# A decoder layer and a gated cross attention on one core: the row sums' spread in one transfer, one step that opens with the values, one copy a quarter earlier

## The reference

```python
# layer 0, hidden x, encoder ctx
q, k, v = split(layernorm(x, ln1) @ w_qkv + b_qkv)          # phase A, 16 heads of 32
x = x + merge(softmax(q k^T / sqrt(32) * mask - 10000 (1 - mask)) v) @ w_ao + b_ao
q = layernorm(x, ln2) @ w_q + b_q;  k, v = split(ctx @ w_kv + b_kv)     # phase B
x = x + merge(softmax(...) v) @ w_co + b_co
x = x + gelu(layernorm(x, ln3) @ w1 + b1) @ w2 + b2         # MLP
# layer 1
a = layernorm(ctx, ln_gamma, ln_beta)
Q, K, V = x @ Wq.T, a @ Wk.T, a @ Wv.T                      # phase D
x = x + tanh(gate) * (merge(softmax(where(mask, Q K^T / sqrt(32), -inf)) V) @ Wo.T)
```

## Time and profile before

| | us |
|---|---|
| median of 3 runs | 1096.38 (1095.52 to 1099.59) |
| profiled execution | 1098.87 |
| its span, first to last instruction | 1097.2 |
| TensorE busy | 1068.6 (97%) |
| VectorE busy | 818.4 (75%) |
| ScalarE busy | 705.3 (64%) |
| GpSimd busy | 481.8 (44%) |

### The profile page before, as it was taken

The page is one execution under the profiler, slowest core; times in us unless marked ns, Lnnn a source line. Parts: engine busy times, 40 slices in busy tenths (PEclk is TensorE's granted clock), DMA queues, the critical chain, the costliest instruction groups (busy, mean ns, idle before and its releaser), DMA issues.

```text
span 1097.2 us, 24221 instructions
## 1 busy us (share of the span) xinstructions
PE 1068.6 (97%) x8741; PEld 924.4 (84%) x8741; DVE 818.4 (75%) x1299; ACT 705.3 (64%) x2354; POOL 481.8 (44%) x361
## 2 busy tenths in 40 slices
PE   7989999999999999999999999999999999999998
PEld 6888888888888888887898888888888988888786
DVE  6677787777888788878867667767697466666667
ACT  4687777777888778787444444444456266666676
POOL 3665656657667766767613122113032222222210
DMA  6365665576677677554243251341647647676611
GB/s 217 102 192 190 212 185 194 175 219 209 214 234 227 203 217 244 159 192 153 82 141 103 69 173 49 125 141 57 206 135 270 211 136 205 204 215 200 200 61 59
DMA packets 145831, 185.92 MB, mean 169 GB/s; under 512 B 17856, under 2 KB 88752, under 8 KB 145712
## 3 DMA queue, kind: packets, MB, share of 16 engines
q1 hardware_dynamic: 145712, 184.37, 53.7%
HBM read 122.59 MB, written 61.73 MB: 168 GB/s over the span
## 4 chain that ended last, share of the span: by engine, by line
PE 39%; DVE 18%; ACT 17%; DMA 7%; POOL 7%; issue 7%; SPq 3%; DVEq 0%; ACTq 0%; POOLq 0%
PE psum L1087 15%; PE psum L1068 14%; POOL prob L2207 6%; ACT prob_blocks L1377 6%; ACT prob L1377 4%; DVE prob L1757 4%; PE psum L890 4%; DVE negmax L1770 3%; ACT second_prob_blocks L1377 3%; DMA normalised<-ln_tile 2%; DVE ln_tile L1692 2%; DVE inputs_transposed L1699 2%; ACT inputs_transposed L1415 2%; PE psum L882 2%; PE psum L1007 1%
## 5 line engine op out<-in xcount | busy, mean ns | idle before, releaser
L890 PE MATMUL psum<-inputs_hi,weights_hi 128*128 128x256 f32 x768 | 224.1, 292 | 5.8 <-POOL inputs_lo L2193 3.5
L890 PE MATMUL psum<-inputs_lo,weights_hi 128*128 128x256 f32 x768 | 217.0, 283 | 0.0
L890 PE MATMUL psum<-inputs_hi,weights_lo 128*128 128x256 f32 x768 | 216.9, 282 | 0.0
L2207 POOL TENSOR_TENSOR prob<-prob,mask_bias 128x1024 f32<-128x1024 f32 x64 | 152.8, 2411 | 98.2 <-DVE prob L1757 96.1
L890 PEld LDWEIGHTS psum<-inputs_hi,weights_hi 128*128 128x128 f32 x768 | 146.6, 191 | 12.7 <-issue 6.0
L1770 DVE TENSOR_REDUCE negmax<-prob 128x8 f32<-128x1024 f32 x96 | 115.6, 1211 | 50.2 <-POOL prob L2207 50.0
L1377 ACT ACTIVATE prob<-prob,negmax 128x128 f32<-128x128 f32 x384 | 148.8, 398 | 0.3 <-DVE negmax L1770 0.3
L890 PEld LDWEIGHTS psum<-inputs_lo,weights_hi 128*128 128x128 f32 x768 | 146.9, 191 | 0.2
L890 PEld LDWEIGHTS psum<-inputs_hi,weights_lo 128*128 128x128 f32 x768 | 146.8, 191 | 0.0
L2193 POOL TENSOR_TENSOR inputs_lo<-inputs_transposed,inputs_hi 128x512 fp32r<-128x512 f32 x70 | 92.9, 1348 | 93.0 <-DVE inputs_hi L1730 61.2
L1377 ACT ACTIVATE prob_blocks<-prob,negmax 128x128 f32<-128x128 f32 x304 | 117.8, 392 | 22.7 <-DVE negmax L1770 22.6
(11 more groups left out here) (132 smaller groups left out, 2657.7 us busy)
## 6 DMA issues: line engine op xcount, KB each, us to landing
prob_turned<-prob_blocks SPq DMA_DIRECT2D x38, 512.0 KB, 3.0
prob<-prob_turned SPq DMA_DIRECT2D x152, 128.0 KB, 3.5
weights_whole<-weights_in SPq DMA_DIRECT2D x72, 256.0 KB, 3.3
inputs_transposed<-normalised SPq DMA_DIRECT2D x120, 128.0 KB, 2.8
normalised<-ln_tile SPq DMA_DIRECT2D x24, 512.0 KB, 2.8
context<-row_sums_spread SPq DMA_DIRECT2D x188, 64.0 KB, 2.1
stream<-residual SPq DMA_DIRECT2D x42, 256.0 KB, 2.9
ln_tile<-stream SPq DMA_DIRECT2D x32, 256.0 KB, 3.8
```

The source lines that it names most:

```text
L890: mm = pe.matmul(ps[:, bank, GT * part:GT * part + GT], w[:, slot, c, o], a[:, buf, c, :], start=c == 0 and i == 0, stop=c == KC - 1 and i ...
L2207: pool.tensor_tensor(half, half, mb.unsqueeze(1).to_broadcast([128, 8, T]), ALU.add).then_inc(s_biased, 1)
```

## The change

It has three parts.

1. The spread of the row sums is one DMA with a source of three dimensions, [4 rows, 32 times, 512], and a destination of 128 partitions, in place of four DMAs of 32 partitions each. Its semaphore now counts 16 an item and not 64.
2. TensorE's step opens with `times_v(g - 2)` also where g - 1 is not in `WHOLE`. Only g = 44 is such a step (42 is in `WHOLE`, 43 is not).
3. In ScalarE's steps with g - 1 in `WHOLE`, 34 to 43, the third half unit is copied after the first quarter of the exponentials and not after the second.

```diff
             def store_row_sums(g):
                 sp.wait_ge(s_rc, g + 1)
                 if g:
-                    sp.wait_ge(s_rsp, 64 * g)
+                    sp.wait_ge(s_rsp, 16 * g)
...
             def spread_row_sums(g):
...
-                for j in range(4):
-                    sp.dma_start(ctxn[32 * j:32 * j + 32, :], spread[j:j + 1, :].to_broadcast([32, KC * T])).then_inc(s_rsp, 16)
+                each = bass.AP(spread.tensor, spread.offset, [[KC * T, 4], [0, 32], [1, KC * T]])
+                sp.dma_start(ctxn[:, :], each).then_inc(s_rsp, 16)
...
-                if st.ends and g - 2 not in WHOLE:
+                if st.ends and (g - 2 not in WHOLE or g - 1 not in WHOLE):
                     times_v(g - 2)
...
-                if g - 2 in WHOLE:
+                if g - 2 in WHOLE and g - 1 in WHOLE:
                     project(*st.units[0], U_BANK, (0,))
                     times_v(g - 2)
                     project(*st.units[0], U_BANK, (1,))
...
                 if g != 28:
                     exps(g, 0)
+                if g - 1 in WHOLE and st.units[2]:
+                    half_out(*st.units[2])
                 exps(g, 1)
-                if st.ends and st.units[2]:
+                if g - 1 not in WHOLE and st.ends and st.units[2]:
                     half_out(*st.units[2])
...
-                dve.wait_ge(s_rsp, 64 * (g + 1))
+                dve.wait_ge(s_rsp, 16 * (g + 1))
```

## The result

The changed kernel takes **1099.55 us** (median of 20 runs, 1097.17 to 1105.2) against 1097.07 for the kernel before (20 runs, 1095.29 to 1100.92): ratio 1.0022, 95% interval 1.0013 to 1.0032. That is +2.5 us where the forecast was +3.4. It lies within the 0.5% that counts as no change, but the interval leaves out 1: the kernel is a little slower. The profiled execution took 1098.95 us, 1097.6 of it the span.

The account below looks back on a forecast made before the run. Several loops of almost equal length run side by side, and a step costs what its longest costs, though TensorE is busiest. Terms 3.05 + 1.5 - 1.2 = +3.35 on the median 1096.4 gave 1100 us; range 1092 to 1110.

Parts of the forecast that it names:

- reading (b): Merged spread of row sums: its outermost count of 4 confines it to four DMA engines, 64 KB each.
- The arrival, 4.5 us: Merged spread: lands 4.5 us after its first issue, taken between 4.0 and 5.3; bounds 2.5 and 6.7.
- my own rival's arithmetic: Rival of four slow engines (23%): spread arrives at 5.5 us, +16.5, 1113; at 5.0 us +9.3, 1106.
- Lateness in A and B (2.65): VectorE's context in items 13, 14, 24, 26: spread late by 0.4, 1.15, 0.2, 0.9 us, counted whole, +2.65.
- The tail (0.4): Items 43 to 45: spread late by 0.3, 0.7, 0.5 us; after idle times only 0.4 of item 44 stays.
- The queue behind the spread (+1.5): SP's queue: three normalised-row stores on the chain land 0.5 us later each, for held engines outweigh earlier issues; +1.5.
- The store named: Store of normalised rows in item 24, issued at 412.85: should land later after issue than the 3.42 us of before.
- Part 2 (-1.2): Item 44's step opens with values: row sums start at 1040.8 in place of 1041.96, -1.2 us; bounds -1.25 and 0.
- The small wait before the values: TensorE in step 44: a new wait of 0.3 us for the second blocks of item 42.
- Part 3 (0): Copy moved in items 34 to 43: TensorE's waits, at most 4.7 us, go, but time stays; 0, bounds -0.8 and +0.6.
- The rival of sixteen engines: Merged spread shared by sixteen DMA engines (20%): nothing late, SP ahead, -3.3 us, 1093.

Follow-up runs that it names:

- e3_sixteen: Changed kernel with the merged spread reading one row 128 times (outermost count 128, some inverse sums wrong): 1094.6 us, 0.9968 of the kernel before.
- e13_early_alone: Kernel before with the merged spread only in 26 items with time in hand (2 to 12, 27 to 41), without parts 2 and 3: 1096.06 us, 0.9986.
- e1_part1: Part 1 alone (merged spread and its two waits) on the kernel before: 1100.14 us, 1.0021.
- e10_early: Changed kernel with the merged spread only in items 2 to 12 and 27 to 41, four old transfers in the others: 1095.27 us, 0.9967 of before.
- e11_early_no_copy: Kernel before with the merged spread only in items 2 to 12 and 27 to 41, and part 2, without part 3: 1094.82 us, 0.9975.
- e12_parts12: Changed kernel with part 3 undone: 1099.31 us, 1.0017 of the kernel before.
- e2_parts23: Parts 2 and 3 on the kernel before, four old transfers kept: 1096.11 us, 0.9989.
- e4_part2: Part 2 alone (TensorE's two conditions) on the kernel before: 1095.71 us, 0.9974.
- e8_replicated: Changed kernel with each inverse sum written four times, so the merged spread reads sixteen right rows on sixteen engines: 1102.39 us, 1.0043 of before.

## Why the prediction was right

The time was right: 1100 forecast, 1099.55 measured. Its mechanism was right in the main: four engines, a spread that comes late, VectorE standing for it. Its sum was right by luck in good part: one term had the wrong sign, one was near by two errors, two were too small or gone, and it started from 1096.4, the median of three runs, where twenty give 1097.07. Step by step:

**Four engines, reading (b): right.** The packets show it, and `e3_sixteen` shows that by this alone the kernel goes from 1.0022 to 0.9968. The Trainium skill's rule ("DMA: Bandwidth & Descriptors", section on why a DMA increments its semaphore by 16) that a transfer uses the largest divisor up to 16 of its slowest counts agrees with both packet counts, 4 and 16 an item. The estimate from that page's figures was 4.3 us (its 2.0 us fixed is fitted to transfers that GpSimd issues, and SP issues this one); the trace has 5.2, and the measurement decides.

**The arrival, 4.5 us: too small.** It is 5.2 (median), and 5.3 at the nine places on the chain. I had scaled 4.0 from the ordinary row and 5.3 from the second blocks' row; the upper one was near. By my own rival's arithmetic (1106 at 5.0, 1113 at 5.5) the time should have been between these two. It was not, so other steps were wrong too. (At 5.5 the rows of before give eight late items in A and B and not the nine that I wrote; their sum of 9.3 is right.)

**Lateness in A and B (2.65): near, by two errors.** The amount was too small because the arrival was. With 5.2 for 4.5 the same sum over the kernel before gives 6.9 us in A and B, and VectorE does wait 6.7 us there, in seven items (12.4 in all, 5.7 of them in the five items of the tail). But counting it whole was too much. Three pairs of kernels differ only in the spread of the 21 items that have no time in hand, and so give its cost without what SP gains elsewhere. Their costs are differences of two ratios, each good to 1.6 to 1.8 us:

| pair | costs, us | of it in the tail | the rest | VectorE waits more in A and B |
|---|---|---|---|---|
| `e13_early_alone` to `e1_part1` | 3.8 | 0.8 | 3.0 | 4.8 |
| `e10_early` to the changed kernel | 6.0 | 2.1 | 3.9 | 5.6 |
| `e11_early_no_copy` to `e12_parts12` | 4.6 | 3.2 | 1.4 | 3.9 |

In sum 8.3 us of 14.3 reach the end, a little over half, 2.8 a kernel. That this is so close to 2.65 is luck. Nor were they the items named: in the changed kernel 13 and 24 don't wait, 14 does (1.48 for the forecast 1.15), 26 by 0.1 only, and items 17, 19, 21, 23 and 25 by 0.4 to 1.0, for which by their places in the kernel before a transfer of 4.5 would have been in time. Item 0 waits 1.0 us, for a transfer of 6.2. With part 1 alone 13, 14 and 26 wait 0.5, 0.5 and 0.6: a wait in one item moves the next.

**The tail (0.4): too small.** Items 42 to 46 wait 1.36, 1.42, 1.22, 0.92 and 0.73, and the tail is longer by 0.8 us without part 2 and by 2.4 with it. I had item 42 arriving in time to the tenth of a microsecond, and nothing left of 43 and 45.

**The queue behind the spread (+1.5): this step failed, the sign is the other one.** The store named landed sooner, beside 3.42 at 412.85 in the earlier trace rows:

```profile
412.82 2.83 DMA normalised<-ln_tile
```

So did the two others, of items 20 and 26: 4.65 and 4.02 us for 4.85 and 5.26. All three were issued within 0.2 us of their old times, since SP now stands there for VectorE's tile, while their spreads were issued 0.9 to 2.1 us sooner (408.01 for 410.10 in item 24). So the stores come 3.9 to 4.8 us behind the spread, when the four engines are nearly done. Closer behind it the delay that I had reckoned with is there: the weights chunk takes 5.2 for 3.3, the mask 5.0 for 2.8, and the stores 1.2, 2.5 and 3.4 us behind a spread (items 0, 14 and 22) take 7.1, 5.0 and 4.5 for 3.9, 3.7 and 3.3. VectorE has no wait for the mask in either kernel, and ScalarE's longest for a chunk is 6.2 us where it was 6.1. What the merged spread does apart from its lateness is measured by `e13_early_alone`, where nothing is late: it is 1.5 us faster than the kernel before. So SP's earlier issues bring more than the held engines cost; the two were not measured apart. I had +1.5.

**Part 2 (-1.2): right by itself, gone in company.** Alone it shortens step 44 by 1.17 us, by the mechanism described; the kernel with it alone is 2.9 us faster, with part 3 1.2. With the merged spread it is worth nothing that can be measured (1.0017 against 1.0021). I had checked only whether the spread of 42 comes in time at 4.5 us. In step 44 the changed kernel keeps little of it, by part 3 and the late spread together; without part 3 the step keeps 1.3 us, and the last items, whose spreads are late too, lose them. The small wait before the values is there: 0.51 and 0.71 us for the forecast 0.3.

**Part 3 (0): right.** In the waits of the changed kernel from 900 to 1036 there is none left for L1324 before L908 or for L1339 before L882 (4.7 us in the earlier trace rows), and the time is the same (0.9999). TensorE ran ahead only until it stood before the row sums, as forecast: in step 43 they start 0.3 us after the inverse sums do, where it was 1.0 in the kernel before. Whether it costs something beside part 2 is not settled: `e2_parts23` is 1.6 us above `e4_part2` (good to 1.5), but `e10_early` 0.9 below `e11_early_no_copy` (good to 1.9).

What was measured of part 1 alone is +2.3 where its terms gave +4.55 (3.05 and 1.5): about 3.0 and 0.8 for the lateness, less 1.5 for SP. Of part 2 in this company it is 0 where I had -1.2. The two errors half cancel, and so 3.35 stood for 2.5.

The rival of sixteen engines would have given 1093, -3.3: `e3_sixteen` measures -3.5 by its ratio (-2.9 by the medians). Its forecast was good, for a transfer that this change doesn't make.

Still open: why part 2 alone brings 2.9 us (1.6 to 3.9) when its step and the tail account for 1.5; why `e12_parts12` loses 1.8 us behind its last row sums; and what in phases A and B lets almost half of VectorE's lateness pass. Nor was any kernel run whose sixteen-engine spread has the right rows at no cost to VectorE.

## What to carry to other kernels

Before merging small broadcasts into one transfer, look at the outermost count of the merged source: it can set how many DMA engines carry it, and the count of packets in the trace tells. A merge saves the issuing queue's time, not the arrival; do it only for the items whose consumer has time in hand, and leave the end of the kernel, where every wait counts, as it is. Two edits that each do well by themselves can cancel: part 2 was worth 2.9 us alone and nothing beside the late spread, which costs most in the tail that part 2 shortens. And before a step's distance is compared between kernels, see whether its first mark has moved too; here one edit moved it by 0.7 us, and a second mark on another engine told another story.

## What the runs showed of the hardware that was not expected

- 256 KB on sixteen engines in one transfer land 3.5 us after the issue starts, no sooner than four transfers of 64 KB issued one behind the other (3.5).
- 256 KB on four engines take 5.2 us (4.65 to 6.6), and the weights chunk and the mask issued right behind them take 1.9 and 2.2 us longer than before; a 512 KB store issued 3.9 to 4.8 us behind them takes no longer.
- An issue takes 337 ns with the two-dimensional source of `e3_sixteen`, 538 with the three-dimensional one on four engines, and 547 in `e8_replicated` with a three-dimensional one whose transfer lands after 3.4: the form of the source, not the number of engines, goes with the longer issue.
- A reciprocal of 128x64 takes 553 ns on VectorE, of 128x16 255.
